# A graph layer with a routed expert layer: thirds for all groups of edges, and another order of the tail

## The chip, the cores and the metric

The kernel runs on one core of a Trainium2 chip. Its engines are PE (matrix products), DVE and ACT (vector work), POOL (here it issues indirect DMAs and little else) and SP (it issues plain DMAs). The metric is the time of the whole kernel on the device in microseconds (us), lower is better.

## What is computed

There are 12500 nodes of 256 features and 212500 edges, sorted by their target.

```python
def reference(x, src, dst, edge_weight, gnn_W, gnn_b, gate_w, gate_b, w1, b1, w2, b2):
    # graph layer: weighted sum over the edges of a node, then a product
    h = layernorm(x)
    agg = segment_sum(h[src] * edge_weight[:, None], dst)        # 12500 x 256
    x = x + agg @ gnn_W.T + gnn_b
    # expert layer: of 8 experts the best one by the gate, with room for ceil(1.25 * 12500 / 8) nodes
    h = layernorm(x)
    probs = softmax(h @ gate_w + gate_b)
    e, prb = argmax(probs), max(probs)
    pos = place of the node in its expert's queue;  kept = pos < C
    y = (relu(h @ w1[e] + b1[e]) @ w2[e] + b2[e]) * prb * kept   # 256 -> 1024 -> 256
    return x + y
```

## The kernel before

**Nodes and edges.** The nodes lie in 98 tiles of 128. The edges lie in 1661 tiles of 128, called columns; 17 columns make a group, one group for each node tile (the last has 12). For each column POOL issues one indirect DMA that gathers 128 rows of features (L744): 204 from x itself for the first 12 groups, whose rows are then normed on the chip, and 1457 from `normed`, which the startup writes.

**Chunks.** The columns of a group are worked off in chunks. The first 12 groups and the last have thirds of 6, 6 and 5 columns, in four buffers; groups 12 to 96 have halves of 9 and 8 columns in three buffers of a ring of 27 columns. For each chunk k there are: `prep` on DVE (one-hot matrices by target, L1342 and L1344), `mm` on PE (the gathered rows times the one-hots, L1002), `pair_out` on ACT (L868), `shift_matrix` on DVE (L1352), `turn` on PE (L1011) and `add` on DVE into the aggregate `aggT` (L1372). POOL waits before a chunk for the products of the chunk that held its buffer, at its fourth column for the add of chunk k - 3 and at its seventh for the products of k - 2.

**Nodes.** When a group is summed, its node tile goes through `gnn` (PE L1042), `x2` (DVE L1419 to L1425: x + agg W, moments), `st` (ACT, the root L829), `nn` (ACT, norm), `tn` (transpose, PE L1055, then ACT L878), `lg` (logits, PE L1062, DVE L1445 to L1452), `ra` and `rk` (ranks within the experts, PE L1071 to L1075, DVE L1462 to L1482) and `rb` (rows sorted by expert, PE L1080, ACT copy L889, stored to the DRAM buffer `tiles_by_expert` at L894). `cp` then copies the tile's rows to the eight experts' queues in DRAM, `rows_by_expert`: eight DMAs of 130 KB by SP (L678, L686), each with a start that SP first loads.

**Visits.** A visit takes 128 rows of one expert's queue through its two layers; there are 105. `plan` (DVE L1494 to L1510) picks the expert. On SP: `hl` loads the rows (`hin`, L639, L656), `wa` the first weights (L665, 1028 KB, only if the expert isn't the one whose weights lie there), `wb` the second (L672, 1152 KB, likewise). `wa` waits for the relu of the visit two before, since its weights lie in the same place. `hn` norms the rows on ACT (`hf`, L901), `tf` transposes them (PE L1086, ACT L906), `l1` is the first product (PE L1094), its halves copied out by ACT (L911), `th` transposes them back (PE L1103), DVE adds the bias (L1515), ACT does the relu (L916), `l2` is the second product (PE L1124) and `z` the result (DVE L1523 to L1525). Visits of the last part take transposed rows that need no copies (PE L1112). The first 89 visits are planned while gathers run (`hl` into `hin`), the rest take their rows into `msg` after the last gather.

**The order.** `schedule_of` writes one list of events; every engine walks through it and does its part of each event, so the list is the order on PE, ACT, DVE and SP alike. There are three slots per group. With halves, the slots of a group in the middle of the run are (numbers: chunk, visit or tile): `l1 47, wa 49, th 47, tn 64` in one; `mm 146, hl 48, cp 63, lg 64, ..., z 47, wb 49, gnn 65` in the next; `mm 147, rb 64, x2 65, st 65, hn 48, nn 65, turn 147, add 147, ..., tf 48` in the third. Three stretches follow each other: dense (visits 0 to 18, one about every 14 us, 574 to 834 us), sparse (one visit per group, 851 to 1608 us) and five visits per four groups (to about 2090 us). Behind the last gather stands a tail with the last nodes' steps (tiles 95, 96 and 97, called c, a and b in `schedule_of`), the pads of the queues (`pads`, eight DMAs, L693 and L696) and the last 21 visits. `HBUFS` is the number of buffers for a visit's rows, here 3.

## Time and profile before

| | us |
|---|---|
| runs before, median of 3 | 2306.87 |
| lowest and highest | 2302.67, 2307.46 |
| the profiled execution, whole time | 2304.34 |
| its span on the core | 2302.5 |
| PE busy, POOL busy in the span | 1777.4, 1701.1 |
| mean granted clock of PE | 0.892 of full |

The profile is of one execution. A group of instructions is told by its line in the code, its engine and what it writes and reads. An engine is idle before an instruction until something releases it, and the profile infers what. "issue" is time in which nothing was waited for. SP and POOL give out DMAs: a row of theirs shows when one is issued and not when it has landed. Where two or more records of the same form follow one another, a row of the timeline joins them and says how many there are (x8).

### The profile page before, as it was taken

Reading aid. Unit: us, or ns where it says so; the run is one execution under the profiler, and the core shown is the slowest. Engines: PE = TensorE matmul, PEld = TensorE weight load, DVE = VectorE, ACT = ScalarE, POOL = GpSimd, SP = SyncE. Lnnn points to the kernel's source line nnn. Section 1 sums busy time; section 2 is a strip of 40 time slices with the busy share of each in tenths; the row PEclk is TensorE's granted clock in tenths of the full one; section 3 lists DMA queues with packets and bytes.
Section 4 is the critical chain, followed back from the end, with each engine's and each line's share of the span. In section 5 each row is a group of like instructions: output and inputs, shape, how many; then the busy total and the mean of one; then the engine's idle time right before and its main releaser. Section 6 shows DMA issues by size and latency. Waiting matters only on the chain.

```text
span 2302.5 us, 36668 instructions
## 1 busy us (share of the span) xinstructions
PE 1777.4 (77%) x9852; PEld 1173.6 (51%) x9852; DVE 1241.0 (54%) x6358; ACT 990.2 (43%) x1941; POOL 1701.1 (74%) x1774
## 2 busy tenths in 40 slices
PE   4444456665999887877887877877988888887899
PEld 3222234343666654545544545545655555555798
DVE  8977433444666555445445445445545555554553
ACT  6777423343555443333333333333444444444222
POOL 7777777777777777777777777777777777775465
PEclk9999985655999998888988888888999999998899
DMA  7766346667777776657557576756776676766478
GB/s 252 230 218 214 115 139 189 197 203 269 237 245 237 242 253 181 206 170 260 168 169 258 166 249 180 243 173 199 235 251 216 180 251 207 257 218 209 138 250 323
DMA packets 172806, 494.76 MB, mean 215 GB/s; under 512 B 48181, under 2 KB 86837, under 8 KB 149894
## 3 DMA queue, kind: packets, MB, share of 16 engines
q0 software_dynamic: 84960, 231.11, 34.0%
q1 hardware_dynamic: 70404, 235.95, 30.2%
q10 hardware_dynamic: 17234, 25.32, 3.0%
q8 instruction: 81, 1.33, 0.2%
q14 instruction: 127, 1.04, 0.1%
HBM read 596.46 MB, written 141.13 MB: 320 GB/s over the span
## 4 chain that ended last, share of the span: by engine, by line
POOL 34%; PE 32%; issue 14%; DVE 11%; ACT 6%; DMA 1%; ACTq 1%; SPq 0%; DVEq 0%; POOLq 0%
POOL msg L744 34%; PE ps L1094 12%; PE ps L1124 11%; PE ps L1112 3%; PE ps L1103 2%; DVE hmid L1515 1%; ACT hmid L916 1%; PE ps L1062 1%; PE ps L1011 1%; ACT hmid L911 1%; ACT hf L901 1%; DVE aggT L1525 1%; DVE st L1423 1%; DVE xrow L1421 1%; DVE onehot L1344 1%
## 5 line engine op out<-in xcount | busy, mean ns | idle before, releaser
L744 POOL DMA_INDIRECT msg<-normed,src_sb x1457 | 1397.8, 959 | 443.9 <-issue 442.3
L1094 PE MATMUL ps<-wsl,hTf 128*128 128x512 f32 x680 | 415.6, 767 | 57.5 <-ACT hTf L906 57.5
L1002 PE MATMUL ps<-msg,onehot 128*32 128x256 f32 x3322 | 312.7, 445 | 164.2 <-DMA msg<-normed,src_sb 94.8
L1124 PE MATMUL ps<-wsl,hmid 128*128 128x256 f32 x1680 | 392.0, 387 | 15.4 <-ACT hmid L916 15.4
L1124 PEld LDWEIGHTS ps<-wsl,hmid 128*128 128x128 f32 x1680 | 314.2, 192 | 65.2 <-issue 25.7
L1515 DVE TENSOR_TENSOR hmid<-ps,wsl 128x512 f32<-128x512 f32 x210 | 142.5, 690 | 342.8 <-PE ps L1103 307.4
L1094 PEld LDWEIGHTS ps<-wsl,hTf 128*128 128x128 f32 x680 | 161.2, 250 | 258.0 <-issue 184.7
L868 ACT COPY pairs<-ps 128x256 f32<-128x256 f32 x208 | 77.4, 372 | 446.4 <-PE ps L1002 436.1
L1002 PEld LDWEIGHTS ps<-msg,onehot 128*32 128x32 f32 x3322 | 116.3, 120 | 287.0 <-DMA msg<-normed,src_sb 109.8
L1011 PE MATMUL ps<-shift,pairs 128*128 128x96 f32 x832 | 167.9, 334 | 109.4 <-ACT pairs L868 108.8
L1372 DVE TENSOR_TENSOR aggT<-aggT,ps 128x192 f32 x208 | 73.5, 353 | 318.8 <-PE ps L1011 301.6
L744 POOL DMA_INDIRECT msg<-in_x,src_sb x204 | 196.8, 965 | 64.1 <-issue 61.5
L1011 PEld LDWEIGHTS ps<-shift,pairs 128*128 128x128 f32 x832 | 136.1, 230 | 182.8 <-ACT pairs L868 177.5
L911 ACT COPY hmid<-ps 128x512 f32<-128x512 f32 x170 | 97.8, 584 | 291.3 <-PE ps L1094 291.3
L916 ACT ACTIVATE hmid<-hmid 128x512 f32<-128x512 f32 x210 | 131.1, 630 | 171.2 <-DVE hmid L1515 171.2
L774 POOL DMA_INDIRECT out_x<-aggT,src_sb x98 | 95.6, 976 | 57.7 <-issue 29.3
L882 ACT ACT_TABLE_LOAD x97 | 124.5, 1283 | 1.7
L829 ACT ACT_TABLE_LOAD x97 | 124.5, 1283 | 1.7
L1042 PE MATMUL ps<-wg_sb,aggT 128*128 128x256 f32 x392 | 118.5, 431 | 0.1
L1103 PE MATMUL ps<-cst,hmid 128*128 128x128 f32 x680 | 101.5, 280 | 13.5 <-ACT hmid L911 13.5
L1103 PEld LDWEIGHTS ps<-cst,hmid 128*128 128x128 f32 x680 | 78.6, 143 | 59.6 <-issue 31.8
L1086 PE MATMUL ps<-cst,hf 128*128 128x128 f32 x210 | 47.7, 313 | 77.1 <-ACT hf L901 77.0
(148 smaller groups left out, 2551.3 us busy)
## 6 DMA issues: line engine op xcount, KB each, us to landing
wsl<-in_wsecond SPq DMA_DIRECT2D x105, 1152.0 KB
wsl<-in_wfirst SPq DMA_DIRECT2D x105, 1028.0 KB
rows_by_expert<-tiles_by_expert SPq DMA_DIRECT2D x752, 130.0 KB
msg<-normed,src_sb POOLq DMA_INDIRECT x1457
xrow<-in_x SPq DMA_DIRECT2D x97, 128.0 KB
wsl<-in_x SPq DMA_DIRECT2D x24, 512.0 KB, 4.0
normed<-wsl ACTq DMA_DIRECT2D x24, 512.0 KB, 3.2
tiles_by_expert<-srow ACTq DMA_DIRECT2D x94, 130.0 KB
```

Of the source, the lines that this page charges most:

```text
L744: pool.indirect_dma_start(out=msg[:, chunk.at + j, :], out_offset=None, in_=x if k < RAW else ln_dram, in_offset=bass.IndirectOffsetOnAxis ...
L829: return nc.scalar.activation(out, variance, ACT.Sqrt, bias=eps[0:out.shape[0], 0:1])
L882: nc.scalar.activation(rt[:, own(n), 2 * E8:3 * E8], rt[:, own(n), E8:2 * E8], ACT.Exp, accum_out=sc[:, own(n), 1:2]).then_inc(s_exp, 1)
L911: nc.scalar.copy(hid_rows[:, half, :], ps[:, H + half, :]).then_inc(s_hid, 1)
L916: nc.scalar.activation(hid_rows[:, half, :], hid_rows[:, half, :], ACT.Relu).then_inc(s_relu, 1)
L1002: last = nc.tensor.matmul(ps[h * QWIN:(h + 1) * QWIN, t % 2, 0:D], onehot[:, j, :], msg[:, j, :], start=i == 0, stop=i == chunk.quarters[h ...
L1011: last = nc.tensor.matmul(ps[:, t % 2, D + k * TWIN:D + (k + 1) * TWIN], pairs[:, t % 2, k * P:(k + 1) * P], shift[:, t % 2, :], start=Tru ...
L1042: last = nc.tensor.matmul(ps[:, x2_bank(n), 0:D], aggT[:, n * P:(n + 1) * P, k], wg_sb[:, k, :], start=k == 0, stop=k == KD - 1)
L1094: last = nc.tensor.matmul(ps[:, H + half, :], hTf[:, k, :], w1_at(v % 2)[:, k, half * HALF * P:(half + 1) * HALF * P], start=k == 0, stop= ...
L1103: last = nc.tensor.transpose(hps(c), hmid[:, c, :], ident)
L1124: last = nc.tensor.matmul(ps[:, Y, 0:D], hmid[:, c, :], w2_at(v % 2)[:, c, :], start=c == 0, stop=c == FC - 1)
L1515: dve.tensor_tensor(hid_rows[:, half, :].rearrange("p (c t) -> p c t", t=P), ps[:, H + half, :].rearrange("p (c t) -> p c t", t=P), b1_at( ...
```

## The change

All groups now have thirds of 6, 6 and 5 columns, in four buffers (24 columns). The tables of chunks of unlike sizes go; there are 293 chunks where there were 208. The list work on DVE (first targets, steps, offsets) that stood in five pieces in slots 1 to 5 for the later groups is done at the start for all. POOL's waits are: the products of the third that held the buffer at a third's start, and its add at the middle column. `cp` moves from the slot six behind a node's start, where it stood behind `hl`, to the slot five behind it, where it is the last but the plans. `HBUFS` is 4. Behind the last gather the events of visits 84 to 88 (and their loads) come ahead of more of the last nodes' steps, and `pads` comes later.

```diff
-HALVES = 3
-HBUFS = 3
+HBUFS = 4
...
     for t in range(-2, real - 1):
-        k = chunk_at.get(t)
-        events.append(("slot", t))
-        if k is not None:
-            events.append(("mm", k))
+        if t >= 0:
+            events.append(("mm", t))
...
-        stage = [starts.get(t - s) for s in range(7)]
+        stage = [starts.get(t - s) for s in range(6)]
         for v, at in queue:
             if at + ROWS_LAG <= t:
                 once("hl", v)
         if stage[4] is not None and stage[4] != c - 1:
             events.append(("rb", stage[4]))
-        if stage[6] is not None and stage[6] < c - 1:
-            events.append(("cp", stage[6]))
...
-        if k is not None:
-            events.append(("turn", k))
-            events.append(("add", k))
+        events.append(("turn", t))
+        events.append(("add", t))
...
         if stage[2] is not None:
             events.append(("tn", stage[2]))
+        if stage[5] is not None and stage[5] < c - 1:
+            events.append(("cp", stage[5]))
...
-    events += [("gnn", a), ("gnn", b), ("ra", c), ("x2", a), ("x2", b), ("rk", c), ("st", a), ("st", b), ("nn", a),
-               ("nn", b), ("rb", c), ("l1", first), ("tn", a), ("tn", b), ("th", first)]
+    events += [("gnn", a), ("gnn", b), ("ra", c), ("x2", a), ("x2", b), ("rk", c), ("st", a), ("st", b), ("rb", c),
+               ("l1", first), ("th", first)]
     for v in plan_at.get(real, ()):
         plan(v, real)
-    events += [("lg", a), ("lg", b)]
     for do in ("hl", "hn", "tf"):
         once(do, second)
-    events += [("l2", first), ("ra", a), ("ra", b), ("z", first), ("rk", a), ("rk", b), ("rb", a), ("rb", b)]
+    events += [("nn", a), ("nn", b), ("l2", first), ("tn", a), ("tn", b), ("z", first), ("lg", a), ("lg", b)]
     queue.pop(0)
     once("hl", queue[1][0])
-    events.append(("pads",))
+    rest()
+    events += [("ra", a), ("ra", b), ("rk", a), ("rk", b), ("rb", a), ("rb", b)]
+    rest()
...
     for _ in range(AHEAD):
         plan_last()
+    rest()
+    rest()
+    events.append(("pads",))
     while pending or queue:
         rest()
...
 def gather(t):
-                    if k >= RAW + HALVES and j == 3:
-                        pool.wait_ge(s_added, k - HALVES + 1)
-                    if k >= RAW + HALVES and j == 6:
-                        pool.wait_ge(*summed(k - HALVES + 1))
+                if t >= RING:
+                    pool.wait_ge(s_mm[u], summed(t - RING))
+                for j in range(SUBS[q]):
+                    if t >= RAW + RING and j == SUBS[q] // 2:
+                        pool.wait_ge(s_added, t - RING + 1)
```

Where the instructions stand. The names in the rows are those above; "waits" lists the semaphores ahead of a row, and line numbers after the change are lower by about 41 on SP and 47 on PE.

SP, in the loop of the sparse stretch, around the load of the rows of visit 48, before: first weights, then the rows, then the copies.

```order
L665 ISA [waits s_relu]
L665 DMA wsl<-in_wfirst 128x2056
L639 TENSOR_LOAD ints [waits s_plan]
L656 ISA [waits s_z,s_scat0,s_scat1]
L656 DMA hin<-rows_by_expert 128x260
L678 TENSOR_LOAD ends_i [waits s_route]
L678 TENSOR_LOAD ends_i
L686 ISA [waits s_bounce,s_scat0]
L686 DMA rows_by_expert<-tiles_by_expert 16x2080
```

The same place after: the copies' start comes right behind the first weights,

```order
L624 ISA [waits s_relu]
L624 DMA wsl<-in_wfirst 128x2056
L637 TENSOR_LOAD ends_i [waits s_route]
L637 TENSOR_LOAD ends_i
L645 ISA [waits s_bounce,s_scat0]
L645 DMA rows_by_expert<-tiles_by_expert 16x2080
```

and behind the last of the eight copies come the rows, the second weights and the load of x.

```order
L645 DMA rows_by_expert<-tiles_by_expert 16x2080
L598 TENSOR_LOAD ints [waits s_plan]
L615 ISA [waits s_z,s_scat0,s_scat1]
L615 DMA hin<-rows_by_expert 128x260
L631 ISA [waits s_z]
L631 DMA wsl<-in_wsecond 128x2304
L579 DMA xrow<-in_x 128x256 [waits s_moved]
```

The load of `hin` has moved from ahead of the eight copies to behind them.

PE, the same loop, from the sorted rows of a tile to the visit's transposes, before:

```order
L1080 MATMUL ps<-xrow,perm 128x260 [waits s_route]
L1086 MATMUL ps<-cst,hf 128x128 [waits s_hf]
L1086 MATMUL ps<-cst,hf 128x128
L1094 MATMUL ps<-wsl,hTf 128x512 [waits s_w1_0,s_hTf]
L1094 MATMUL ps<-wsl,hTf 128x512 x3
L1103 MATMUL ps<-cst,hmid 128x128 [waits s_hid]
L1103 MATMUL ps<-cst,hmid 128x128 x3
L1103 MATMUL ps<-cst,hmid 128x128 [waits s_hid]
L1103 MATMUL ps<-cst,hmid 128x128 x3
L1055 MATMUL ps<-cst,hrow 128x128 [waits s_sorted,s_h]
```

and after:

```order
L1033 MATMUL ps<-xrow,perm 128x260 [waits s_route]
L1039 MATMUL ps<-cst,hf 128x128 [waits s_hf]
L1039 MATMUL ps<-cst,hf 128x128
L955 MATMUL ps<-msg,onehot 32x256 [waits s_added,s_msg3]
L955 MATMUL ps<-msg,onehot 32x256 x4
L1047 MATMUL ps<-wsl,hTf 128x512 [waits s_w1_0,s_hTf]
L1047 MATMUL ps<-wsl,hTf 128x512 x3
L964 MATMUL ps<-shift,pairs 128x96 [waits s_shift,s_pair]
L964 MATMUL ps<-shift,pairs 128x96
L1056 MATMUL ps<-cst,hmid 128x128 [waits s_hid]
L1056 MATMUL ps<-cst,hmid 128x128 x3
```

A part of a third's product now stands between the transposes of hf and the first layer, and a turn between the first layer and its transposes; the transposes themselves stand in the same order.

SP behind the last gather, before: the pads begin behind the load of rows of visit 86.

```order
L656 ISA [waits s_z,s_scat1,s_scat0]
L656 DMA hin<-rows_by_expert 128x260
L693 TENSOR_LOAD pad_i [waits s_scat1,s_padrow]
L696 ISA
L696 DMA rows_by_expert<-in_pads 16x2080
```

After, they begin behind the second weights of visit 88,

```order
L631 ISA [waits s_z]
L631 DMA wsl<-in_wsecond 128x2304
L652 TENSOR_LOAD pad_i [waits s_scat1,s_padrow]
L655 ISA
L655 DMA rows_by_expert<-in_pads 16x2080
```

and the last of them stands right ahead of the load of the rows of that visit.

```order
L655 ISA
L655 DMA rows_by_expert<-in_pads 16x2080
L598 TENSOR_LOAD ints [waits s_plan]
L615 ISA [waits s_z,s_put1,s_put0]
L615 DMA hin<-rows_by_expert 128x260
```

The pads have moved behind two more visits' weights and one more load of rows, to the place directly ahead of the load for visit 88.

## Rows read from the trace of the kernel before

**Rows 1.** The page, busy time (share of the span) and instructions of each engine:

```profile
PE 1777.4 (77%) x9852; PEld 1173.6 (51%) x9852; DVE 1241.0 (54%) x6358; ACT 990.2 (43%) x1941; POOL 1701.1 (74%) x1774
```

**Rows 2.** What POOL waited for, from its wait list: us in total, times, longest:

```profile
POOL msg L744 <- issue: 503.9, 1654, 0.3
...
POOL msg L744 <- DVE aggT L1372: 1.5, 5, 0.3
```

**Rows 3.** Windows: length, PE, PEld, DVE, ACT, POOL busy, clock, DMA share, GB/s:

```profile
574.00:834.00 260.00, 240.21 (x1418) 167.80 (x1417) 167.23 (x890) 138.12 (x269) 197.40 (x206) 0.99 0.76 244
853.00:1609.00 756.00, 616.95 (x3290) 378.32 (x3290) 370.00 (x1937) 289.11 (x560) 573.39 (x600) 0.87 0.65 200
```

**Rows 4.** Timeline of POOL: start, duration, what, idle before and releaser; two gathers:

```profile
1608.73 0.95 POOL L744 DMA_INDIRECT msg<-normed,src_sb  x1 [0.30 <-DVE aggT L1372]
...
2102.06 0.95 POOL L744 DMA_INDIRECT msg<-normed,src_sb  x1 [0.30 <-issue]
```

**Rows 5.** The line of hf in the sparse stretch: count, first and last start:

```profile
L901 ACT ACTIVATE hf<-hin x36: 583/585/599, 851.2 to 1607.7; 128x256 f32<-128x256 f32 x36
```

**Rows 6.** Timeline of ACT, hf five visits apart in the 5/4 stretch:

```profile
1691.95 0.58 ACT L901 ACTIVATE hf<-hin 128x256 f32<-128x256 f32 x1
...
1774.40 0.58 ACT L901 ACTIVATE hf<-hin 128x256 f32<-128x256 f32 x1
```

**Rows 7.** Timeline of ACT, one loop of the sparse stretch:

```profile
1401.68 0.63 ACT L916 ACTIVATE hmid<-hmid 128x512 f32<-128x512 f32 x1 [0.27 <-DVE hmid L1515]
...
1412.92 0.29 ACT L829 ACTIVATE sd<-mv,eps 128x1 f32<-128x1 f32 x1 [1.32 <-DVE mv L1424]
1413.12 0.58 ACT L901 ACTIVATE hf<-hin 128x256 f32<-128x256 f32 x1
...
1424.10 0.63 ACT L916 ACTIVATE hmid<-hmid 128x512 f32<-128x512 f32 x1 [0.27 <-DVE hmid L1515]
```

**Rows 8.** Timeline of PE, the same loop, first transposes of the visit's rows:

```profile
1413.76 0.44 PE L1086 MATMUL ps<-cst,hf 128*128 128x128 f32 x2 [1.58 <-ACT hf L901]
```

**Rows 9.** Timeline of SP, the same loop:

```profile
1402.62 0.08 SPq L665 DMA_DIRECT2D wsl<-in_wfirst  x1
1403.28 0.34 SPq L656 DMA_DIRECT2D hin<-rows_by_expert  x1
1405.08 6.00 SPq L686 DMA_DIRECT2D rows_by_expert<-tiles_by_expert  x8
```

**Rows 10.** Timeline of SP in the dense stretch:

```profile
656.08 6.01 SPq L686 DMA_DIRECT2D rows_by_expert<-tiles_by_expert  x8
662.71 0.34 SPq L672 DMA_DIRECT2D wsl<-in_wsecond  x1
663.66 0.33 SPq L656 DMA_DIRECT2D hin<-rows_by_expert  x1
```

**Rows 11.** Timeline of ACT, hf after the load of rows 10:

```profile
671.85 0.60 ACT L901 ACTIVATE hf<-hin 128x256 f32<-128x256 f32 x1 [4.13 <-DMA hin<-rows_by_expert]
```

**Rows 12.** The chain that ended last, in the tail: start, length, what:

```profile
2151.57 2.14 DMA hin<-rows_by_expert
...
2160.90 6.92 DMA hin<-rows_by_expert
```

**Rows 13.** The page's groups (count, busy, mean ns, idle before), turns on PE:

```profile
L1011 PE MATMUL ps<-shift,pairs 128*128 128x96 f32 x832 | 167.9, 334 | 109.4 <-ACT pairs L868 108.8
```

**Rows 14.** Timeline of PE in the tail, its two large holes:

```profile
2127.91 0.66 PE L1055 MATMUL ps<-cst,hrow 128*128 128x128 f32 x2 [7.09 <-ACT pairs L873]
...
2168.49 0.69 PE L1086 MATMUL ps<-cst,hf 128*128 128x128 f32 x2 [6.23 <-ACT hf L901]
```

**Rows 15.** Timeline of SP in the tail, the pads:

```profile
2139.85 7.91 SPq L696 DMA_DIRECT2D rows_by_expert<-in_pads  x8
```

**Rows 16.** Timeline of DVE in the tail, the last add but one:

```profile
2110.90 0.35 DVE L1372 TENSOR_TENSOR aggT<-aggT,ps 128x192 f32 x1 [0.95 <-PE ps L1011]
```

**Rows 17.** Timeline of DVE at the start, steps of the first lists:

```profile
15.92 1.19 DVE L1218 TENSOR_TENSOR rel<-rel,wsl 128x24 f32<-128x24 f32 x12
```

More of the change, by code:

```diff
@@ L312, in gnn_moe_kernel @@
     HALF = FC // 2
-    NT, G, CHUNKS, RCOLS, NC, QUEUE, REAL_COLS = (sizes[q] for q in (
-        "tiles", "group", "chunks", "ring", "columns", "queue", "edge_tiles"))
-    T = len(CHUNKS)
+    NT, G, SUBS, NC, QUEUE, QUARTERS, REAL = (sizes[q] for q in (
+        "tiles", "group", "subs", "columns", "queue", "quarters", "real"))
+    T = 3 * NT
     COLS = NT * G
-    LONGEST = max(c.size for c in CHUNKS)
+    OFF = [0, SUBS[0], SUBS[0] + SUBS[1]]
+    QOFF = [[OFF[q] + sum(QUARTERS[q][:h]) for h in range(4)] for q in range(3)]
     LAST_ROWS = N - (NT - 1) * P
@@ L534, in rows_of, with third, arrived, summed @@
             return LAST_ROWS if n == NT - 1 else P
-        def arrived(k):
-            return s_msg[CHUNKS[k].buffer], CHUNKS[k].arrived
-        def summed(k):
-            return s_mm[CHUNKS[k].buffer], CHUNKS[k].used
-        def column(k):
-            return CHUNKS[k].group * G + CHUNKS[k].start
-        def quarter(k, h):
-            return sum(CHUNKS[k].quarters[:h])
-        def added_for(n):
-            return sum(c.group <= n + 1 for c in CHUNKS)
-        SPANS = [(0, 3, 0, RAW_GROUPS), (RAW, 2, RAW_GROUPS, NT - 1),
-                 (RAW + 2 * (NT - 1 - RAW_GROUPS), T - RAW - 2 * (NT - 1 - RAW_GROUPS), NT - 1, NT)]
+        def third(t):
+            g, q = divmod(t, 3)
+            return g, q, t % RING, (t % RING) * SUBS[0]
+        def arrived(t):
+            return 16 * sum(SUBS[k % 3] for k in range(t % RING, t + 1, RING))
+        def summed(t):
+            return 4 * (t // RING + 1)
         def ln_tiles(b):
@@ L988, in aggregate @@
             def aggregate(t):
-                chunk = CHUNKS[t]
+                g, q, u, m = third(t)
                 if t < RAW:
@@ L1202, in _ @@
             link.mark(dve.memset(flat[:, top - DVE_ZERO // 2:top], 0.0))
-            rel3 = rel[:, :].rearrange("p (g j) -> p g j", j=G)
-            def heads(some, h):
-                dve.wait_ge(s_prepe, h + 1 if some.start == 0 else h + 5)
-                link.mark(dve.tensor_copy(firsts[:, h, some], ps[:, (0 if some.start == 0 else IN) + h, some]))
-            def bases(some):
-                link.mark(dve.tensor_copy(base_i[:, some], firsts[32:33, 0, some]))
-            def steps(span, q):
-                first, parts, low, high = SPANS[span]
+            for q in range(3):
+                dve.wait_ge(s_prepe, q + 1)
+                link.mark(dve.tensor_copy(firsts[:, q, :, :], ps[:, H + q, 0:4 * NT].rearrange("p (h g) -> p h g", h=4)))
@@ L1214, in steps @@
+            link.wait()
+            link.mark(dve.tensor_copy(base_i.rearrange("p (g q) -> p q g", q=3), firsts[32:33, :, 0, :]))
+            rel3 = rel[:, :].rearrange("p (g j) -> p g j", j=G)
+            for q in range(3):
                 for h in range(4):
-                    n, start = CHUNKS[first + q].quarters[h], CHUNKS[first + q].start + quarter(first + q, h)
-                    part = rel3[:, low:high, start:start + n]
-                    head = firsts[:, h, first + q:first + q + parts * (high - low - 1) + 1:parts]
@@ L1565, in _ @@
                     general()
-                    for t in range(RAW, RAW + 2):
+                    for t in range(RAW, RAW + 3):
                         prep(t)
```

239 lines of the change are left out of this document (88 added, 151 removed).

## The prediction

> **What bounds the kernel now.** I read the page's busy times first, then what POOL waited for, then the windows by stage, and last one loop of the middle stage engine by engine. PE is busy for 1777 us and POOL for 1701 us of a span of 2302.5 us [rows 1]; an average says nothing on who sets the end, since the stages differ. The wait list of POOL shows what held the gathers (L744): nearly all of the idle time before them is "issue", 0.3 us a time; adds of the aggregate held one 5 times, for 1.5 us in all [rows 2]. So up to the last gather the kernel runs at POOL's pace. In the sparse stretch, 853 to 1609 us, 600 gathers took 756 us [rows 3]: 1.26 us each, 21.42 us for the 17 of one group. The last gather is issued at 2102.06 [rows 4]; behind it stands a tail of 200 us, bound by PE and by what PE waits for.
>
> How near is anything else to taking POOL's place? In the sparse stretch each group of 17 columns comes with one visit, and the 36 norms of visits' rows (hf, L901) from 851.2 to 1607.7 make 35 periods of 21.61 us [rows 5]. That is 0.2 us **more** than POOL's 21.42: the visits' loop falls behind POOL all through the stretch, by 35 x 0.2 = 7 us in all, and at 1608.73 a gather is released by an add [rows 4]. The margin is used up just as the stage ends. From there five visits come per four groups, and they take 1774.40 - 1691.95 = 82.45 us [rows 6] against POOL's 4 x 21.42 = 85.7, so the loop recovers. Whatever is added to the loop of the sparse stretch has next to no cover.
>
> **The loop, step by step.** It closes on itself: relu of a visit ends (I call this R), SP loads what the next visits need, a visit's rows are normed (hf), transposed, multiplied by the first weights, relu. One turn: R at 1401.68 + 0.63 = 1402.31, hf at 1413.12, next R at 1424.10 + 0.63 = 1424.73 [rows 7]. R to hf is 10.81 us; hf to R is 21.61 - 10.81 = 10.80 on average. What holds hf at 1413.12 is the root before it on ACT, which DVE's chain released at 1412.92, and not its rows: SP issued hin at 1403.28, right behind the (skipped) load of weights at 1402.62 [rows 9], and a load of hin with nothing ahead lands after 2.14 us [rows 12]. The rows lie ready some 7 us early.
>
> **The change, part by part.**
>
> *The copies ahead of the rows.* The step that copies a tile's rows to their queues goes from behind the load of hin to a place ahead of it; the order fences of the change show both. SP issues in order, and the weights' load ahead of both waits for R, so the copies can't start earlier than now. Worked out: the weights' load ends at 1402.70. From hin's end (1403.62) to the first copy (1405.08) are 1.46 us now [rows 9], so the first copy goes out at 1404.16; eight of them take 6.00 us, to 1410.16; the next issue behind copies comes 0.62 us on (662.09 to 662.71, [rows 10]), so hin goes out at 1410.78. Then the landing, which has bounds: 2.14 us with nothing ahead, and 8.19 us (663.66 to 671.85, ACT waiting for it) with eight copies and 1.15 MB of weights ahead [rows 10, 11]. At the 244 GB/s that this stage moved [rows 3] those weights alone are 4.7 us, so copies alone would leave about 3.5; I take 3.6, an estimate nearer to the lower end, since in the sparse stretch DMA is busy for 0.65 and not 0.76 [rows 3]. hf then stands at 1414.38, **R to hf 12.07 instead of 10.81**: +1.25. The ends: nothing (with 2.14 the rows land at 1412.92, with the root) and +5.9.
>
> Where the first weights are really reloaded (10 of the 36 visits), 1.05 MB go out ahead of copies and rows. No row shows that case. It costs from 0 to the 4.3 us that 1.05 MB are at 244 GB/s; I take 2.5, since SP spends 8 us on the copies before hin is even issued, on average 10/36 x 2.5 = **+0.7**.
>
> The Trainium skill, "DMA: Bandwidth & Descriptors", section "Anatomy of one DMA — SWDGE (gpsimd) path", gives each DMA a fixed cost of about 2.0 us plus its bytes over 436 GB/s, which would be 2.3 us for these rows. That agrees with the 2.14 alone and knows no queue; by it this part is all but free, which is rival A. The same page's "Queues, rings and completion order" has a row's DMAs share rings that are worked off in order, and ACT's wait of 4.13 us for hin behind other loads [rows 11] is on that side.
>
> *Thirds instead of halves.* One chunk more per group. It brings on PE one more turn (L1011: 167.9 us for 208 of them, 0.81 us busy [rows 13]), on ACT a copy of the pairs, on DVE a shift and an add. On PE most of it falls into waits that stand there (1.58 us before L1086 in the loop shown [rows 8]), but one turn now stands between a visit's first products and their transposes, inside hf to R: **+0.25**, between 0 and 0.81. The ring shrinks from 27 columns to 24, but a third is freed after 6: before as after POOL may run some 20 gathers, 25 us, ahead of an add.
>
> So the loop takes 21.6 + 1.25 + 0.7 + 0.25 = **23.8 us** against POOL's 21.42. That is 2.38 x 35 = 83 us, less the margin with which the stretch is entered, 7 us today and taken as 8. Stretch: **+75**.
>
> *The stretch with five visits per four groups.* Two of five visits have the sparse order: 82.45 + 2 x 1.95 + 4 x 0.25 = 87.35 against 85.7, and (2086 - 1620) / 85.7 = 5.4 rounds: 5.4 x 1.65 = **+9** (0 to 16).
>
> *The start of the tail.* The last add but one ends at 2110.90 + 0.35 = 2111.25 [rows 16], 16.7 us behind the gather that it needs (2094.5, six before the last). A loop that holds POOL back stands at the limit of 25 to 26 us: **+9**.
>
> *The tail.* The same products in another order. Today PE has two large holes in it, 7.09 us for x and 6.23 us for the rows of visit 88 [rows 14]; the load of these goes out at 2160.90 and lands 6.92 on, with weights ahead [rows 12]. The new order issues the products of visits 85 to 87 ahead of more of the last nodes' steps, which fills part of the first. But the eight pad copies, 7.91 us on SP and today at 2139.85, 13 us clear of that load [rows 15], now stand directly ahead of it, behind the second weights of 88: it goes out some 8.7 us later against its weights, and about 5 of these are covered by visit 87's products. Less what the first hole gives back, net **+4** (-6 to +9). The fourth row buffer lifts a wait of the load of hin on s_z that comes last for none of these loads: 0.
>
> *Startup.* The list work that later slots did for groups 12 to 97 goes to the front, ahead of the first one-hots. Twelve steps on 24 elements take 1.19 us there today [rows 17]; the new ones have up to 196. **+1** (0 to 5), since the products wait for the gathered rows and not for DVE until some 28 us.
>
> Sum: 75 + 9 + 9 + 4 + 1 = 98. The profiled execution took 2304.34 us, 2.5 under the median of 2306.87; on its own time that is 2402, and 2405 on the median. I take **2403**.
>
> **The rivals.**
>
> A, the copies cost hin nothing: it lands 2.14 to 2.3 us after issue and the root still holds hf. The loop is 21.6 + 0.25 = 21.86, (21.86 - 21.42) x 35 - 8 = 7 us of it reach POOL and part is recovered; with 1 to 4 for the tail 2308 to 2316. For it is the landing of 2.14; against it the 8.19. Chance 0.08.
>
> B, the same mechanism at a smaller price. TensorE's granted clock was 0.87 of full in this stretch [rows 3], a mix of its two levels; a loop that waits more may run its products at either; and a reload may hide under the copies' 8 us on SP. Loop 22.1 to 22.4: 35 x 0.7 to 1.0 - 8 = 16 to 27, nothing in the next stretch, the tail's start 2 to 5, the tail 4: 2328 to 2342. Chance 0.17.
>
> C, the other side, **faster**: rows land early as in A, the thirds free buffers soon enough that POOL never waits, and the pieces of visits 85 to 87 fill both holes of the tail, 7.09 and 6.23 us, of which 2 are lost to startup and turns: 13.3 - 2 = 11 at most, 6 if one is half filled: 2296 to 2301. It decides from a hin load landing within 2.2 us behind copies and a load for visit 88 that is out before PE runs dry. Against it: the pads right ahead of that load. Chance 0.04.
>
> D, the change doesn't do what it says: the fourth row buffer lets no load start earlier, since SP's order and the plan hold it. That is in my sum already and changes no time.
>
> E, dearer than summed: hin lands as at 8.19 in every loop, which is 28 us: above 2440. Chance 0.06.
>
> **The numbers.** Forecast 0.65, its own range 2360 to 2438 (landing 2.8 to 4.5, reload 0 to 4.3, tail -6 to +9). B 0.17, A 0.08, C 0.04, E 0.06. The range for 8 in 10 goes from the lower end of B to just above the forecast's own: 2328 to 2440. A measurement of this kernel tells some 0.2%, 4.6 us, from no change. Faster: C, 0.04. Within: the lower part of A, 0.05. Slower: the rest, 0.91.
>
> **What would show it.** In the profile of the changed kernel: hf 23 to 24.5 us apart in the sparse stretch instead of 21.61; ACT idle before hf until DMA hin; the eight copies on SP between first weights and hin; tens of us of POOL's time before L744's counterpart for adds or products; the last gather near 2185 instead of 2102; less POOL in the chain. Wrong would be hf still released by DVE's chain and gathers idle for "issue" alone: then it is A. With the gathers' end near 2125 it is B. If the last gather comes where it did and the end has moved, only the tail matters; if the load for 88 isn't behind the pads by the trace, my tail term falls.

## The result and the profile after

The changed kernel took 2441.19 us (median of 4 runs, 2432.74 to 2447.0) where the kernel before took 2307.16: a ratio of 1.0572, 95% interval 1.0545 to 1.0599. Its profiled execution has a span of 2445.1 us, 142.6 more than the 2302.5 of before. The forecast was 2403, a ratio of 1.042; the range reached to 2440, and the time lies at its very end (the median is 1 us above it; the ratio times the median of before, 1.0572 x 2306.87 = 2438.8, is a little below).

Where the 142.6 us lie is read from the issue of the same gathers in both traces: counted from 0, gather 612 opens the 37th group and gather 1292 the 77th.

| up to | before | after | added in this stretch | forecast |
|---|---|---|---|---|
| gather 612 (start, dense stretch) | 778.2 | 812.3 | 34.1 | 1 |
| gather 1292 (sparse stretch) | 1636.5 | 1753.0 | 82.4 | 75 |
| last gather (five visits per four groups) | 2102.1 | 2225.7 | 7.1 | 9 |
| end of the span (tail) | 2302.5 | 2445.1 | 19.0 | 9 + 4 |

The page after, busy times and chain, answers [rows 1]. PE and DVE have more to do in a longer span; in the chain that ended last stand SP (SPq, 19%) and DMA (13%), and POOL holds 17% where it had 34%. The last line is the chain of before.

```profile
PE 1883.1 (77%) x10160; PEld 1229.5 (50%) x10160; DVE 1297.4 (53%) x6670; ACT 1016.5 (42%) x2026; POOL 1698.2 (69%) x1774
...
PE 30%; SPq 19%; POOL 17%; DMA 13%; issue 11%; ACT 5%; DVE 5%; DVEq 0%; ACTq 0%; POOLq 0%
```

```profile
POOL 34%; PE 32%; issue 14%; DVE 11%; ACT 6%; DMA 1%; ACTq 1%; SPq 0%; DVEq 0%; POOLq 0%
```

POOL's wait list, against [rows 2]: adds now hold gathers 101 times for 150.3 us, where it had been 1.5.

```profile
POOL msg L701 <- DVE aggT L1292: 150.3, 101, 3.9
```

The windows of the dense and the sparse stretch, against [rows 3] (length, busy times of PE, PEld, DVE, ACT, POOL, clock, DMA share, GB/s): in the dense one the DMA engines moved 208 GB/s instead of 244, in the sparse one 190 instead of 200, so nothing here points to bandwidth as the limit. PE was busy for less of the dense stretch (228.35 us where it was 240.21) and its granted clock there was 0.90 where it was 0.99.

```profile
574.00:834.00 260.00, 228.35 (x1219) 156.06 (x1218) 148.26 (x811) 117.22 (x233) 171.43 (x180) 0.90 0.66 208
853.00:1609.00 756.00, 594.80 (x3155) 364.98 (x3153) 361.44 (x1905) 275.01 (x548) 520.49 (x546) 0.86 0.61 190
```

The line of hf (the norm of a visit's rows on ACT) from visit 18 to visit 54, against [rows 5]: 36 periods from 872.0 to 1725.7, **23.71 us** each instead of 21.61. The forecast had 23.8.

```profile
L857 ACT ACTIVATE hf<-hin x37: 599/599/601, 872.0 to 1725.7; 128x256 f32<-128x256 f32 x37
```

One loop of the sparse stretch, against [rows 7] to [rows 9]. SP: first weights, eight copies, rows.

```profile
1521.60 0.08 SPq L624 DMA_DIRECT2D wsl<-in_wfirst  x1
1523.13 6.11 SPq L645 DMA_DIRECT2D rows_by_expert<-tiles_by_expert  x8
1530.18 0.35 SPq L615 DMA_DIRECT2D hin<-rows_by_expert  x1
```

ACT of the same loop: relu, root, hf, next relu.

```profile
1520.07 1.23 ACT L872 ACTIVATE hmid<-hmid 128x512 f32<-128x512 f32 x2 [0.99 <-DVE hmid L1435]
...
1531.83 0.29 ACT L783 ACTIVATE sd<-mv,eps 128x1 f32<-128x1 f32 x1 [1.34 <-DVE mv L1344]
1534.01 0.60 ACT L857 ACTIVATE hf<-hin 128x256 f32<-128x256 f32 x1 [1.88 <-DMA hin<-rows_by_expert]
...
1543.98 1.23 ACT L872 ACTIVATE hmid<-hmid 128x512 f32<-128x512 f32 x2 [0.99 <-DVE hmid L1435]
```

R, the end of a visit's relu, is 1520.07 + 1.23 = 1521.30; hin goes out at 1530.18 and hf, which waits 1.88 us for its load, starts at 1534.01: R to hf is 12.71 us (forecast 12.07) and next R, 1543.98 + 1.23 = 1545.21, comes 11.20 later (forecast 11.05). The root is done 1.9 us before the rows are there. It is so in every loop of the stretch: in all 35 from visit 19 to visit 53 ACT stands idle before hf until the load of hin, for 0.98 to 4.56 us. PE, the same loop:

```profile
1534.66 0.69 PE L1039 MATMUL ps<-cst,hf 128*128 128x128 f32 x2 [3.58 <-ACT hf L857]
1535.28 1.92 PE L955 MATMUL ps<-msg,onehot 128*32 128x256 f32 x10
1537.13 5.24 PE L1047 MATMUL ps<-wsl,hTf 128*128 128x512 f32 x8
```

PE waits 3.58 us for hf where it waited 1.58 in [rows 8]. Then the ten products of the third take 1.92 us and the first layer 5.24; what these take otherwise is shown in the experiments.

In the dense stretch the copies stood ahead of the rows before the change too [rows 10]. What is new there is the load of x. Before, it went out ahead of the copies; SP before the change:

```profile
709.64 0.08 SPq L665 DMA_DIRECT2D wsl<-in_wfirst  x1
709.77 0.34 SPq L620 DMA_DIRECT2D xrow<-in_x  x1
711.55 6.41 SPq L686 DMA_DIRECT2D rows_by_expert<-tiles_by_expert  x8
```

Now it goes out behind them. SP after the change:

```profile
722.05 0.08 SPq L624 DMA_DIRECT2D wsl<-in_wfirst  x1
723.56 6.39 SPq L645 DMA_DIRECT2D rows_by_expert<-tiles_by_expert  x8
730.00 0.58 SPq L579 DMA_DIRECT2D xrow<-in_x  x1
```

and DVE, which waits for that x before it can norm the node (L1339):

```profile
734.11 0.42 DVE L1339 TENSOR_TENSOR xrow<-xrow,bg_sb 128x256 f32<-128x256 f32 x1 [3.68 <-DMA xrow<-in_x]
```

x goes out at 730.00, behind eight copies that began at 723.56, and DVE starts on it at 734.11. In the list of what DVE waited for between 570 and 880 us this stands 13 times, 35.9 us; before it stood there not at all.

```profile
DVE xrow L1339 <- DMA xrow<-in_x: 35.9, 13, 3.8
```

The tail, against [rows 14] and [rows 15]. SP issues the second weights of visit 88, the eight pads, and then the rows of visit 88, and PE is idle 10.15 us for them instead of 6.23:

```profile
2297.89 0.34 SPq L631 DMA_DIRECT2D wsl<-in_wsecond  x1
2298.79 8.09 SPq L655 DMA_DIRECT2D rows_by_expert<-in_pads  x8
2307.45 0.35 SPq L615 DMA_DIRECT2D hin<-rows_by_expert  x1
```

```profile
2310.30 0.69 PE L1039 MATMUL ps<-cst,hf 128*128 128x128 f32 x2 [10.15 <-ACT hf L857]
```

### The profile page after: what moved, and what is told of

It is laid out like the page before. It is cut to its first block, busy times and chain, and to the rows that moved or that the text cites. A ratio compares the mean times of both kernels' runs of the same rounds, so it can differ in the third digit from the quotient of the medians.

```text
span 2445.1 us, 38064 instructions
## 1 busy us (share of the span) xinstructions
PE 1883.1 (77%) x10160; PEld 1229.5 (50%) x10160; DVE 1297.4 (53%) x6670; ACT 1016.5 (42%) x2026; POOL 1698.2 (69%) x1774
## 4 chain that ended last, share of the span: by engine, by line
PE 30%; SPq 19%; POOL 17%; DMA 13%; issue 11%; ACT 5%; DVE 5%; DVEq 0%; ACTq 0%; POOLq 0%
POOL msg L701 17%; SPq L645 14%; PE ps L1047 12%; DMA hin<-rows_by_expert 9%; PE ps L1077 5%; PE ps L955 4%; ACT hmid L872 3%; SPq L637 3%; PE ps L1065 3%; DMA xrow<-in_x 3%; DVE hmid L1435 2%; DMA rows_by_expert<-tiles_by_expert 2%; PE ps L1039 2%; PE ps L964 1%; ACT hf L857 1%
## 5 line engine op out<-in xcount | busy, mean ns | idle before, releaser
L955 PE MATMUL ps<-msg,onehot 128*32 128x256 f32 x3322 | 414.5, 486 | 135.0 <-ACT msg L817 59.8
L1292 DVE TENSOR_TENSOR aggT<-aggT,ps 128x192 f32 x293 | 103.6, 354 | 711.8 <-PE ps L964 690.5
L1047 PE MATMUL ps<-wsl,hTf 128*128 128x512 f32 x680 | 379.6, 709 | 0.9
L964 PE MATMUL ps<-shift,pairs 128*128 128x96 f32 x1172 | 223.6, 321 | 104.6 <-ACT pairs L824 102.6
L824 ACT COPY pairs<-ps 128x256 f32<-128x256 f32 x293 | 109.1, 372 | 464.9 <-PE ps L955 455.4
L964 PEld LDWEIGHTS ps<-shift,pairs 128*128 128x128 f32 x1172 | 189.9, 223 | 210.3 <-ACT pairs L824 175.3
L955 PEld LDWEIGHTS ps<-msg,onehot 128*32 128x32 f32 x3322 | 135.2, 125 | 299.4 <-issue 119.2
L1047 PEld LDWEIGHTS ps<-wsl,hTf 128*128 128x128 f32 x680 | 149.3, 232 | 206.3 <-issue 200.7
L1039 PE MATMUL ps<-cst,hf 128*128 128x128 f32 x210 | 55.9, 358 | 185.8 <-ACT hf L857 185.5
L1039 PEld LDWEIGHTS ps<-cst,hf 128*128 128x128 f32 x210 | 28.1, 171 | 209.7 <-ACT hf L857 209.0
```

The source lines that it names most:

```text
L955: last = nc.tensor.matmul(ps[h * QWIN:(h + 1) * QWIN, t % 2, 0:D], onehot[:, j, :], msg[:, j, :], start=i == 0, stop=i == QUARTERS[q][h] - 1)
L964: last = nc.tensor.matmul(ps[:, t % 2, D + k * TWIN:D + (k + 1) * TWIN], pairs[:, t % 2, k * P:(k + 1) * P], shift[:, t % 2, :], start=Tru ...
L1039: last = nc.tensor.transpose(ps[:, IN, k * P:(k + 1) * P], hf[:, k * P:(k + 1) * P], ident)
L1047: last = nc.tensor.matmul(ps[:, H + half, :], hTf[:, k, :], w1_at(v % 2)[:, k, half * HALF * P:(half + 1) * HALF * P], start=k == 0, stop= ...
```

## The experiments

Theory 1: the place of the copies on SP's queue costs the time, since loads of rows and of x go out and land behind them. Theory 2: the 85 chunks more cost it, in the loop and by the smaller ring. What follows rests on six runs, beside which the kernel before took 2305 to 2309 us; six others, beside which it took 2961 and 2962 us, stand at the end of this section. "Beside" gives the time of the kernel before on the same chip.

**Undo the move of the copies.** In the changed kernel:

```diff
...
-        stage = [starts.get(t - s) for s in range(6)]
+        stage = [starts.get(t - s) for s in range(7)]
...
             events.append(("rb", stage[4]))
+        if stage[6] is not None and stage[6] < c - 1:
+            events.append(("cp", stage[6]))
...
-        if stage[5] is not None and stage[5] < c - 1:
-            events.append(("cp", stage[5]))
```

> The same kernel as e1_copies_back (the changed one with the copies back behind the load of hin), once more, since in that first set the kernel before took 2961 us where it had taken 2307 and all engines stood idle between instructions with nothing to wait for. Theory 1 (place of the copies): 2310 to 2325 beside a kernel before of 2307, last gather 2102 to 2110. Theory 2 (the 85 chunks more): 2400 or more.

Measured: 2304.63 us beside 2305.1, ratio 1.0002 (0.9992 to 1.0012). The last gather came at 2099.3, which is 126 us earlier than in the changed kernel. The whole loss is gone, and with the 85 chunks more the kernel isn't slower than before. It went below the 2310 to 2325 that were expected. One of the fastest loops in its trace, ACT:

```profile
1401.56 0.58 ACT L857 ACTIVATE hf<-hin 128x256 f32<-128x256 f32 x1
...
1409.09 1.23 ACT L872 ACTIVATE hmid<-hmid 128x512 f32<-128x512 f32 x2 [0.99 <-DVE hmid L1435]
...
1420.99 0.58 ACT L857 ACTIVATE hf<-hin 128x256 f32<-128x256 f32 x1
```

R (1409.09 + 1.23 = 1410.32) to hf is 10.67, close to the 10.81 of before; but hf to R is 8.76, where it was 10.80 on average before and never under 10.08. PE of the same loop:

```profile
1402.19 0.44 PE L1039 MATMUL ps<-cst,hf 128*128 128x128 f32 x2 [1.58 <-ACT hf L857]
1402.56 1.05 PE L955 MATMUL ps<-msg,onehot 128*32 128x256 f32 x10
1403.77 3.70 PE L1047 MATMUL ps<-wsl,hTf 128*128 128x512 f32 x8 [0.16 <-ACT hTf L862]
```

The ten products of a third stand between the transposes of hf and the first layer, take the place of a wait of 1.14 us on ACT's hTf, and the first layer runs its eight products in 3.70 us. In the loop of [rows 7] hf to R was 11.61 us; there the same eight products took 6.67. In the changed kernel's loop above, PE waits 3.58 us instead of 1.58, and the products behind that wait take 1.92 and 5.24 us instead of 1.05 and 3.70. The granted clock (the third number from the end) was at the lower level there and at full in the loop of this kernel:

```profile
1534.00:1538.00 4.00, 3.34 (x13) 1.35 (x14) 1.31 (x11) 2.10 (x5) 3.09 (x4) 0.50 0.50 139
```

```profile
1404.00:1408.00 4.00, 4.00 (x15) 2.09 (x15) 0.94 (x5) 1.09 (x3) 3.09 (x4) 1.00 0.47 135
```

This is one loop of each, and the one of this kernel is among its best. Its first layer takes 3.70 us in 13 of the 35 loops from visit 19 to 53 and up to 5.9 us in the others, also in loops with the same wait of 1.58 us; the changed kernel never gets below 4.0. The granted clock of the window 880 to 1600 us is 0.92 in this kernel, 0.87 in the one before and 0.86 in the changed one. The averages over the 35 loops, read from ACT's timelines, are these (the two columns add up to the time of a loop):

| mean of 35 loops, us | R to hf | hf to R |
|---|---|---|
| before | 10.82 | 10.79 |
| halves, the copies moved (next experiment) | 12.55 | 11.02 |
| the changed kernel | 12.69 | 11.08 |
| thirds, the copies back (this experiment) | 11.06 | 10.41 |

With thirds and the copies back, the visits' loop can be faster than POOL (19.43 us in the loop shown, against 21.42), and then it is POOL that sets the pace: in the window 880 to 1600 us PE waits 26 times for gathered rows, 27.6 us in all, and not once in the kernel before or the changed one. How fast the loop would be without POOL, on average, the trace can't show.

**The move of the copies alone**, in the kernel before:

```diff
-        if stage[6] is not None and stage[6] < c - 1:
-            events.append(("cp", stage[6]))
...
             events.append(("tn", stage[2]))
+        if stage[5] is not None and stage[5] < c - 1:
+            events.append(("cp", stage[5]))
```

> The same kernel as e2_copies_moved_alone (the kernel before with only the copies moved), once more for the same reason. Theory 1: 2400 to 2430 beside 2307, sparse period 23.3 to 24. Theory 2: within 20 us of the kernel before.

Measured: 2430.57 beside 2305.1, ratio 1.0535 (1.0497 to 1.0574). One event put one slot earlier gives nearly all of the 5.7%, with halves and with the old tail. hf came 23.52 us apart (872.6 to 1719.2, 36 periods). With halves POOL is held by the products of the chunk before last and not by adds:

```profile
POOL msg L744 <- PE ps L1002: 137.3, 49, 6.6
```

These two runs settle the cause: the loss needs the move of the copies, and the move alone gives 5.35 of the 5.72%. No run puts the rows ahead of the copies with the copies left in their new slot; that it is the rows that come late is read from ACT's wait for hin in each of the 35 loops, and from the run with half the copies below.

**x ahead of the copies.** To part the dense stretch from the sparse one, the changed kernel issues each load of x one tile ahead:

```diff
+            loaded = {0, 1}
+            def once_x(n):
+                if n < NT and n not in loaded:
+                    loaded.add(n)
+                    load_x(n)
             for kind, *key in EVENTS:
-                if kind == "rb" and key[0] + 2 < NT:
-                    load_x(key[0] + 2)
+                if kind == "rb":
+                    once_x(key[0] + 2)
                 elif kind == "cp":
+                    once_x(key[0] + 3)
                     copy_rows(key[0])
```

> The same kernel as e4_x_ahead: the changed one with each load of x one tile ahead and issued ahead of the eight copies. If x behind the copies is what the dense stretch loses: POOL's gather 612 (36 groups) comes near 778 to 786 instead of 812.3, DVE no longer waits for x there, the sparse stretch keeps 23.7 us a visit but is entered with the margin of some 8 us, and the whole is 2400 to 2418 beside 2305. If the dense stretch is bound by the rows or the turns: 2435 to 2445.

Measured: 2409.45 beside 2309.0, ratio 1.0423 (1.0398 to 1.0449). Gather 612 is at 776.3 (778.2 before, 812.3 in the changed kernel): the 34 us of the dense stretch are gone. The sparse stretch is as slow as in the changed kernel, hf 824.9 to 1685.0, 23.9 us apart. SP in the dense stretch now:

```profile
694.32 0.08 SPq L624 DMA_DIRECT2D wsl<-in_wfirst  x1
694.45 0.34 SPq L579 DMA_DIRECT2D xrow<-in_x  x1
696.22 6.43 SPq L645 DMA_DIRECT2D rows_by_expert<-tiles_by_expert  x8
```

DVE no longer waits for x there. This is the kernel that the forecast had described without knowing it: 2409 measured, 2403 foretold, ratio 1.0423 against 1.042.

**Half the copies ahead.** Four of the eight go ahead of the rows, four behind them in the next slot:

```diff
             events.append(("rb", stage[4]))
+        if stage[6] is not None and stage[6] < c - 1:
+            events.append(("cq", stage[6]))
...
-                for e in range(E8):
+                for e in range(4 * half, 4 * half + 4):
...
-                    copy_rows(key[0])
+                    copy_rows(key[0], 0)
+                elif kind == "cq":
+                    copy_rows(key[0], 1)
```

> The changed kernel with four of the eight copies of a tile ahead of the load of hin and four behind it in the next slot. By the sum of the prediction hin goes out 3.1 us earlier than with eight ahead (four issues of 0.77 us), near R + 5.5, and lands 1.5 to 2 us before DVE's root would let hf start, and x likewise. If hf is held by whichever comes last, half the copies cost almost nothing and not half: sparse period 21.4 to 21.9, the whole 2303 to 2325. If each copy ahead costs its share (queueing, SP's time, bandwidth): half of 136, 2365 to 2380.

Measured: 2311.38 beside 2309.0, ratio 1.0007 (0.9995 to 1.0019). Half the dose costs nothing that can be measured, where a share for each copy would have been half of 5.7%, some 66 us. SP and ACT of one loop:

```profile
1410.86 0.08 SPq L626 DMA_DIRECT2D wsl<-in_wfirst  x1
1412.39 2.91 SPq L647 DMA_DIRECT2D rows_by_expert<-tiles_by_expert  x4
1415.89 0.89 SPq L617 DMA_DIRECT2D hin<-rows_by_expert  x1
```

```profile
1409.31 1.23 ACT L876 ACTIVATE hmid<-hmid 128x512 f32<-128x512 f32 x2 [0.99 <-DVE hmid L1439]
...
1421.02 0.29 ACT L787 ACTIVATE sd<-mv,eps 128x1 f32<-128x1 f32 x1 [1.28 <-DVE mv L1348]
1421.22 0.59 ACT L861 ACTIVATE hf<-hin 128x256 f32<-128x256 f32 x1
```

hin goes out at 1415.89, 5.35 us behind R (1409.31 + 1.23), and hf follows the root at once. The rows and DVE's chain are two arms of one wait: the rows cost nothing until they come last. With eight copies they came last in every loop, by 1.9 us in the one shown.

**Thirds without the new tail.** In the kernel of the first experiment the order behind the last gather is that of before (the lines with + and - of the change's tail turned round).

> Thirds for all groups and the fourth row buffer, with the copies behind the load of hin and the tail of before. Against e5_copies_back_2 it undoes only the order of the tail, whose last gather came at 2099.3 (2102.1 before) and whose tail took 6 us more than before from there. If the new order of the tail costs these: 2297 to 2300 beside 2305. If the tail only starts behind a later lag and its order is neutral: 2303 to 2306.

Measured: 2302.91 beside 2309.0, ratio 0.9974 (0.9965 to 0.9984). That is faster than before by 0.26%. The same kernel with the new tail had 1.0002, so the new tail costs 0.28%, some 6 us. The hole ahead of visit 88 in the kernel with the new tail (SP, then PE):

```profile
2158.99 8.52 SPq L655 DMA_DIRECT2D rows_by_expert<-in_pads  x8
2168.08 0.35 SPq L615 DMA_DIRECT2D hin<-rows_by_expert  x1
```

```profile
2171.75 0.69 PE L1039 MATMUL ps<-cst,hf 128*128 128x128 f32 x2 [11.39 <-ACT hf L857]
```

and PE's two holes with the order of before:

```profile
2121.37 0.41 PE L1004 MATMUL ps<-cst,hrow 128*128 128x128 f32 x2 [2.39 <-ACT pairs L825]
...
2159.49 0.69 PE L1035 MATMUL ps<-cst,hf 128*128 128x128 f32 x2 [6.54 <-ACT hf L853]
```

The pads directly ahead of the load for visit 88 make 11.39 us of 6.54. In the profiled executions the time from the last gather to the end is 206.5 us with the new tail and 191.3 with the old; the second was the fastest of its ten runs, so that the 6 us by the medians are the better measure.

**Both holes.** From the last kernel, two things were moved on SP: x of the last two node tiles ahead of the last copies, and the rows of visits 87 and 88 right behind those of 86, ahead of the pads, for which the fourth row buffer is needed.

```diff
                 elif kind == "cp":
+                    if key[0] == COPIED - 1:
+                        once_x(key[0] + 3)
+                        once_x(key[0] + 4)
                     copy_rows(key[0])
...
-    once("hl", queue[1][0])
+    for v, _ in queue[1:]:
+        once("hl", v)
     events.append(("pads",))
```

> A candidate to beat both: e8 with the loads of x for the last two node tiles issued ahead of the last copies, and the loads of hin for visits 87 and 88 right behind that of 86, ahead of the pads, as the fourth row buffer allows. PE's holes of 7.09 us (x) and 6.23 us (rows of 88) should shrink to 0 to 3 us each. If both are on the path: 2287 to 2293. If the pads, now later, or DVE's ranks take their place: no better than e8, 2297 to 2300.

Measured: **2283.06 beside 2309.0, ratio 0.9891 (0.9873 to 0.9909)**, faster than both kernels and 4 us under the lower end of what was expected. SP issues two loads of x before the copies and three of rows before the pads:

```profile
2106.99 0.93 SPq L576 DMA_DIRECT2D xrow<-in_x  x2
2109.60 5.98 SPq L642 DMA_DIRECT2D rows_by_expert<-tiles_by_expert  x8
...
2129.28 2.35 SPq L612 DMA_DIRECT2D hin<-rows_by_expert  x3
2132.28 8.61 SPq L652 DMA_DIRECT2D rows_by_expert<-in_pads  x8
```

and of PE's holes only small ones are left, two of which are:

```profile
2123.03 0.44 PE L1046 MATMUL ps<-cst,hf 128*128 128x128 f32 x2 [1.28 <-ACT hf L864]
...
2134.37 3.69 PE L1084 MATMUL ps<-wsl,hmid 128*128 128x256 f32 x16 [1.98 <-ACT hmid L879]
```

From the last gather to the end PE is idle for 7.2 us in all, where it was 17.8 in the run before. That is 10.6 of the 20 us between the two medians (13.7 between the two profiled spans); where the rest comes from is open, and so is what each of the two moves is worth, since none ran by itself.

**The runs on two slower chips.** Six runs were made on two chips where the kernel before took 2961 us (2946 to 2978) and 2962 us (2926 to 2990) and not 2305. The trace of the first of them shows engines idle for a releaser that the profile can only call remote, on ACT, DVE and POOL alike, and POOL held by adds although the copies are behind the rows:

```profile
ACT pairs L824 <- remote: 420.3, 101, 12.6
POOL msg L701 <- DVE aggT L1292: 416.4, 145, 6.8
```

There a visit comes every 27 us even with the copies behind the rows, so the loop is longer than POOL's pace for another reason, and where the copies stand matters little. The four kernels with thirds take 0.6% to 1.5% less there than the kernel before, wherever their copies stand, and the two with halves the same as it. Why these chips were slow is open. The first four of these runs:

> The changed kernel with the copies of a tile's rows back behind the load of hin, in the slot six behind the node's start. Theory 1 (the place of the copies on SP costs the time, since rows and x queue behind them): the last gather returns from 2225.7 to 2102 to 2110, hf in the sparse stretch follows DVE's root again 21.4 to 22.0 us apart, and the whole is 2310 to 2325, what remains being the new order of the tail. Theory 2 (the 85 chunks more cost it, by their turns, pair copies and adds in the visits' loop and by the smaller ring): 2400 or more. A mixture would lie between, and the sparse period tells how much.

Measured: 2941.06 beside 2961.32, ratio 0.9927 (0.989 to 0.9963).

> The kernel before, halves and its own tail, with only the copies moved to the end of the slot five behind the node's start. Theory 1: sparse period 23.3 to 24, POOL waits for adds for over 100 us, last gather 2200 to 2225, the whole 2400 to 2430. Theory 2: within 20 us of the kernel before, since no chunk is added.

Measured: 2957.94 beside 2961.32, ratio 0.9981 (0.9944 to 1.0018). By its letter this would speak for theory 2; the same kernel beside a before of 2305 gave 1.0535.

> The changed kernel with the order of the tail of before (pads behind the load for visit 86). By the traces, visit 84 starts 11.5 us later against the last gather and the load for visit 88 stands behind the pads, where PE waits 10.15 us instead of 6.23. If the tail's order costs, the whole falls by 4 to 9 us, to 2432 to 2437, and the hole ahead of visit 88 shrinks to 6 to 7 us. If the tail's extra time only comes from the lag with which the loop enters it, the whole stays within 3 us of 2441.

Measured: 2930.18 beside 2961.32, ratio 0.9884 (0.9811 to 0.9958). The changed kernel itself did not run on this chip, so the tail's share in it isn't known from here; the run of thirds without the new tail answers it for the kernel with the copies back.

> The changed kernel with each load of x one tile ahead, issued by SP ahead of the eight copies instead of behind them. In the trace of the changed kernel DVE waits 13 times for x in the dense stretch, 35.9 us in all, and POOL has lost 34 us by the end of it. If the loads of x behind the copies are the cause there, the dense stretch costs 0 to 8 us instead of 34, DVE no longer waits for x, and the whole is 2405 to 2418; the sparse stretch keeps its 23.7 us. If the dense stretch is bound by the turns or by the rows, x ahead changes nothing: 2436 to 2446.

Measured: 2920.83 beside 2961.32, ratio 0.9854 (0.9795 to 0.9914). It doesn't say what x ahead is worth, for the same reason. The last two ran on the second such chip:

> The changed kernel with three buffers for the visits' rows instead of four. If no load of rows ends on that wait, as the prediction's rival D has it: within 5 us of the changed kernel, 2432 to 2446 beside 2305 (ratio 1.055 to 1.060). If the fourth buffer lets rows in earlier anywhere, the loads of hin come later and the whole is 2450 or more.

Measured: 2934.31 beside 2962.03, ratio 0.9942 (0.9902 to 0.9982). HBUFS was 3 in it and nothing else changed. Without the changed kernel beside it, it doesn't say what the fourth buffer is worth. The trace of the changed kernel does: with three buffers a load of rows would wait for the result of the visit three before, and every one of these loads goes out at least 16.9 us after that result. The fourth buffer lets no load start earlier in it.

> The kernel before (halves, three row buffers, copies behind the rows, its own tail) with only the loads moved that e10_both_holes moved: x of the last two node tiles ahead of the last copies, the rows of visit 87 ahead of the pads and those of 88 as soon as its buffer is free. It asks whether the gain of e10 (2283 beside 2309) is the loads' or the thirds'. If the loads': 2288 to 2296 beside 2305, holes of 7.09 and 6.23 us down to 0 to 3 each. If the thirds or the fourth buffer are needed for it: 2300 to 2306.

Measured: 2956.01 beside 2962.03, ratio 0.9998 (0.9953 to 1.0043). Its edits are those of the kernel with both holes, made in the kernel before with its three row buffers. It stays open what the loads alone would bring there.

## Why the prediction was right, and where not

*What bounds the kernel* was right: the visits' loop in the sparse stretch had next to no cover, and POOL waited for adds as soon as it grew (150.3 us).

*The copies ahead of the rows* was the right cause, and the one that the experiments single out: 1.0535 of 1.0572 with that edit alone, 1.0002 without it. Its terms, in the loop shown: the first copy at R + 1.83 (forecast 1.85), hin out at R + 8.88 (8.47; the copies took 6.11 and not 6.00, and SP needed 0.94 us behind them and not 0.62), and hf starts 3.83 us later (3.6 taken, between 2.14 and 8.19). Over the 26 of the 35 loops without a reload that last time is 3.67 us on average, and R to hf 12.44 (forecast 12.07). The landing was the term with the widest bounds, and the estimate from the weights' share held.

*The rule of the Trainium skill* ("DMA: Bandwidth & Descriptors", "Anatomy of one DMA — SWDGE (gpsimd) path"), from which the prediction took an estimate of 2.3 us for a DMA of these rows, is given there for DMAs that POOL issues, and SP issues these. It agreed with the 2.14 us of [rows 12]. Behind eight copies the trace doesn't agree with it: hf starts 3.83 us after the issue.

*The reload* was taken at +2.5 us for a visit. The nine reloads in the 35 loops have R to hf 13.42 on average, against 12.44 without: +0.98, or 0.25 a loop where the forecast had 0.7. The term was too dear by some 0.4 us a loop, and the copies' own term too cheap by as much (12.44 against 12.07), so that R to hf came out at 12.69 against 12.07 + 0.7 = 12.77. That the two misses cancel is luck.

*Thirds instead of halves*, +0.25 us a loop, held for the changed kernel: with the copies moved, the loop is 23.71 us with thirds and 23.52 with halves, and hf to R is 11.08 on average against 10.80 + 0.25 = 11.05. What it rested on was incomplete. I had priced the turn that comes in and not the ten products that move into a wait of PE. With the copies back these show: hf to R falls to 8.76 in the best loops and is 10.41 on average, under the 10.79 of before. In the changed kernel, where PE waits longer for the rows and then runs at the lower clock in the loop shown, nothing of it is left. So the move of the copies costs halves 1.7 us by the rows and 0.2 in hf to R; with thirds it also takes away what they would give, which is 2.4 us from the best loop (11.20 against 8.76) and not known on average.

*The dense stretch* is the step that failed: the forecast put it at nothing, and it cost 34.1 us, a quarter of the loss. I walked the copies past the load of hin only, and had read SP's order for x in the sparse loop alone, where x goes out behind the copies before and after. In the dense stretch the copies stood ahead of hin already; what they pass there is the load of x, which had gone out ahead of them, and DVE has to wait for it before it can norm the node (35.9 us in 13 waits). The run with x ahead gives it back: with it the forecast's sum is off by 6 us. No term of the sum covers these 34 us, so that the time still lies at the end of the range is luck too.

*The margin* of 8 us wasn't there in the changed kernel, since the dense stretch had used it up. In the run with x ahead, which has it, the sparse stretch costs 78 us and not 82, against 75 in the forecast.

*The start of the tail and the tail*: the last add but one ends 25.9 us behind the gather that it needs, as forecast, instead of 16.7; visit 84's rows are normed 23.2 us behind the last gather instead of 11.7, +11.5 (forecast 9), and from there to visit 88's it is +6.7 (forecast 4). Both mechanisms are seen in the trace; with the copies back, the tail's new order costs 6 us by the medians.

*Startup*: the twelve steps took 3.07 us instead of 1.19 and the first one-hots began 4.65 us later (22.80 for 18.15), and POOL had lost 1.7 us after four groups and 0.4 after 28: the estimate of 1 held.

*The rivals.* A (the copies cost nothing) and C (faster) fall by the two traces; B's smaller price falls by 23.71 us a loop. E (above 2440) falls as a mechanism by R to hf: 12.69 us on average and 15.39 at most, where hin landing as late as in [rows 11] would have given some 17. D's mechanism is confirmed by the trace of the changed kernel, where with three buffers no load of rows would have waited (each goes out 16.9 us or more after the result it would need); its run beside the slow kernel before gives no time for it. In the run with both holes the fourth buffer is used: the load for visit 88 goes out 7.8 us before the result of visit 85. My range was cut too low at the top because no rival held "the move hits another stage as well".

## What to carry to other kernels

When a block of DMAs is moved on a queue, list every load that it passes in every stage of the program, not in one: the same move passed the rows in one stage and x in another, and each cost where it came last. A load costs nothing while another arm of the same wait comes later, so ask for the moment at which it becomes the last and test it with half the dose. And read a loop's PE times at the clock that it gets, and over many turns: the same eight products took 3.70 us in 13 of 35 loops of one kernel and up to 5.9 in the others.

## What was not expected of the hardware

- The same eight products of the first layer took 3.70 us in a loop at full clock, 5.24 in the changed kernel's, where the granted clock was 0.50 as they began, and 6.67 in the kernel before. With one and the same wait of PE ahead (1.58 us) they took from 3.70 to 5.8 us within one kernel, so that the wait alone doesn't tell the clock.
- Splitting eight copies of 130 KB into four ahead and four behind a load took the whole delay away; SP needed 0.75 us for each.
- On two of the chips the whole program, the kernel before included, took 28% longer (2961 against 2307 us), with engines idle and 420 us of ACT's time before L824 put down to a remote releaser. A comparison made there (0.9981) would have cleared the edit that costs 5% elsewhere.
